# Linear stage of a two-layer conditioned transformer: biases carried by one channel of the norm's output, and another order of stages

## What is computed

```python
# layer 0: adaptive norm, attention with 16 heads of 16 channels, feed-forward 256 -> 1024 -> 256
x = x + attention(_ln(x) * (scale1 + 1) + shift1) * gamma1
x = x + fc2(gelu(fc1(_ln(x) * (scale2 + 1) + shift2))) * gamma2
# layer 1: linear attention
xn = layer_norm(x, norm_g, norm_b)
q = (xn @ Wq + bq); k = (xn @ Wk + bk); v = (xn @ Wv + bv)     # 16 heads of 16 channels
q = softmax(q, over the channels of a head); k = softmax(k, over the tokens)
y = q @ (k.T @ v)                                              # per sequence and head
h = layer_norm(y, sn_g, sn_b) * (1 + scale) + shift
return x + cond * (silu(h) @ out_W + out_b)
```

## Time and profile before

| | us |
|---|---|
| median of three runs | 1304.96 |
| the profiled execution | 1303.32 |
| its span, first to last instruction | 1301.6 |
| TensorE busy (matmuls) | 1165.3 (90%) |
| VectorE busy | 989.4 (76%) |
| ScalarE busy | 802.9 (62%) |
| GpSimd busy | 845.0 (65%) |
| mean granted TensorE clock | 0.971 of full |

### The profile page before, as it was taken

How to read it: one execution, slowest core, us unless ns; L and a number is a source line. 1 busy time by engine, 2 the same in 40 slices (tenths; PEclk the granted TensorE clock), 3 DMA queues, 4 the chain that set the end, 5 groups by cost and what they waited for, 6 DMA issues and landing times. The chain is left out here.

```text
span 1301.6 us, 37761 instructions
## 1 busy us (share of the span) xinstructions
PE 1165.3 (90%) x12137; PEld 838.6 (64%) x12290; DVE 989.4 (76%) x2338; ACT 802.9 (62%) x2144; POOL 845.0 (65%) x1018
## 2 busy tenths in 40 slices
PE   4687999999999964999999999986999999999996
PEld 3466777777777753566666666663666666666663
DVE  6787999999999836656555556435899999999984
ACT  2676778778877741635454544523676776776764
POOL 4567777777777744546666667542476676676667
PEclk8899999999999986999999999997999999999999
DMA  8542222222222221110101010100011111111112
GB/s 277 143 129 49 56 60 59 59 61 56 58 58 61 62 51 53 26 24 17 33 16 32 16 32 17 33 17 1 17 39 38 40 52 37 40 52 39 44 50 74
DMA packets 138368, 67.73 MB, mean 52 GB/s; under 512 B 76352, under 2 KB 137024, under 8 KB 138304
## 3 DMA queue, kind: packets, MB, share of 16 engines
q1 hardware_dynamic: 109904, 40.92, 12.4%
q10 hardware_dynamic: 28400, 25.99, 6.9%
HBM read 41.18 MB, written 8.65 MB: 38 GB/s over the span
## 5 line engine op out<-in xcount | busy, mean ns | idle before, releaser
L1124 PE MATMUL f_ps_y<-w_fc,f_h_split 128*128 128x256 bf16 x1536 | 172.7, 273 | 2.3 <-DVE f_branch L1243 2.3
L1151 PE MATMUL f_ps_h<-f_x_split,w_fc 128*128 128x512 bf16 x737 | 166.5, 383 | 4.5 <-DVE f_biases L1277 1.4
L1124 PEld LDWEIGHTS f_ps_y<-w_fc,f_h_split 128*128 128x128 bf16 x1536 | 150.2, 98 | 23.6 <-issue 3.0
L657 POOL TENSOR_TENSOR e_split<-e_full,e_split 128x1024 bf16<-128x1024 f32 x64 | 136.6, 2134 | 40.0 <-ACT e_full L730 40.0
L1251 DVE TENSOR_TENSOR f_h_split<-f_h,f_h_split 128x512 bf16<-128x512 f32 x64 | 64.2, 1006 | 104.3 <-ACT f_h L1110 104.3
L1151 PEld LDWEIGHTS f_ps_h<-f_x_split,w_fc 128*128 128x128 bf16 x768 | 75.5, 99 | 89.1 <-issue 3.4
L1109 ACT ACTIVATE f_h_split<-f_ps_h,columns 128x512 bf16<-128x512 f32 x128 | 89.2, 697 | 66.5 <-POOL f_h_split L1066 36.4
L790 PE MATMUL ps_s<-qk_t,k_pairs 128*128 128x64 bf16 x3072 | 102.1, 194 | 29.0 <-DMA k_pairs<-qk_t 25.8
L790 PEld LDWEIGHTS ps_s<-qk_t,k_pairs 128*128 128x128 bf16 x3072 | 97.3, 99 | 37.2 <-issue 19.8
L1066 POOL TENSOR_TENSOR f_h_split<-f_h,f_h_split 128x512 bf16<-128x512 f32 x64 | 79.8, 1257 | 36.7 <-ACT f_h L1110 36.7
L1455 POOL TENSOR_TENSOR l_rstd<-l_mean_var,eps_norm 128x2 f32<-128x2 f32 (+1 forms) x73 | 14.3, 196 | 136.9 <-DVE l_mean_var L1648 107.0
(11 more groups left out here) (187 smaller groups left out, 3233.2 us busy)
## 6 DMA issues: line engine op xcount, KB each, us to landing
v_pairs<-v_split SPq DMA_DIRECT2D x128, 66.0 KB, 2.1
k_pairs<-qk_t SPq DMA_DIRECT2D x256, 32.0 KB, 2.2
gain<-gammas SPq DMA_DIRECT2D x64, 128.0 KB, 3.0
f_gain<-gammas ACTq DMA_DIRECT2D x32, 256.0 KB, 4.3
l_gate<-in_cond ACTq DMA_DIRECT2D x128, 64.0 KB, 2.5
out<-x_all ACTq DMA_DIRECT2D x16, 512.0 KB, 3.0
x_all<-in_x SPq DMA_DIRECT2D x13, 512.0 KB, 5.4
fc_full<-in_L_cond_fc_w SPq DMA_DIRECT2D x2, 1024.0 KB, 7.5
```

Of the source, the lines that this page charges most:

```text
L657: pool.tensor_tensor(flat(e_split[a][:, LO]), flat(e_full[:]), flat(e_split[a][:, HI]), ALU.subtract).then_inc(e_lo_made, 1)
L1124: last = pe.matmul(ps_y[:, i], h_split[a][:, hs, f, i * P:(i + 1) * P], m.w_fc2[:, ws, f], start=(f == 0 and k == 0), stop=(f == F_CHUNKS ...
L1151: last = pe.matmul(ps_h[f % 4][:], m.w_fc1[:, ws, c, f * P:(f + 1) * P], x2_split[a][:, xs, c], start=(k == 0 and c == 0), stop=(k == 2 an ...
```

## The change

The first channel of x_hat is no longer written by the norm but held at one: two memsets ahead of the linear stage set it in both buffers, and hat writes channels 1 to 255, with both sides cut into rectangles (5x51 and 3x85). Since x_hat adds up to zero, channel 0 is minus the sum of the others; so the first weight row, times its gain, is subtracted from all the others, and its own place in the weights is taken by the bias. The three bias matmuls per tile and bias_rows' last three parts go. The high and low halves carry the bias like any weight row.

For that, feed_forward_pass loads the first rows of the three matrices to all partitions (three more DMAs, and one for the first gain), VectorE scales them and folds them into the weights, gain included, in float32 (four scalar_tensor_tensor of L1267's kind), and puts the biases into row 0; ScalarE's high half is one copy of 1536 columns, VectorE's low half one subtraction.

In linear_pass the four lists of stages have another order. TensorE's turn_x comes behind qkv and q_kv; VectorE's x3_low behind v_low, and k_low and mask at the end; ScalarE's modulate near the front and k_high, q_copy behind the exponentials; GpSimd's silus ahead of the deviations. The lags stay. Two waits are new: qkv for q_lower of the tile ahead, and v_low for v_high; hat waits for the memsets once.

The diff, cut to its core (the parameter and semaphore declarations are left out, and the waits for the loads, which count ten instead of six):

```diff
--- before.py
+++ after.py
@@ -150,9 +150,8 @@
         self.ones = sb("ones", [P, P], BF16)
-        self.bias_rows = sb("bias_rows", [P, 5 * C], BF16)
-        self.rows_proj, self.rows_out3, self.rows_qv3, self.rows_k3 = (
-            self.bias_rows[:, a * C:b * C] for a, b in ((0, 1), (1, 2), (2, 4), (4, 5)))
+        self.bias_rows = sb("bias_rows", [P, 2 * C], BF16)
+        self.rows_proj, self.rows_out3 = (self.bias_rows[:, a * C:(a + 1) * C] for a in range(2))
 
...
@@ -959,7 +959,8 @@
         biases3 = sb("biases3", [P, 3 * C], F32, 1)[0]
-        biases3_high, biases3_mid = m.w_qkv[:, HI, 0, :], m.w_qkv[:, HI, 1, :]
+        first_rows = sb("first_rows", [P, 3 * C], F32, 1)[0]
+        first_gain = sb("first_gain", [P, 1], F32, 1)[0]
         b_norm3_wide = m.fc_full[:, 6 * C:6 * C + NC_ * P].rearrange("p (c n) -> p c n", c=NC_)
...
@@ -1024,6 +1028,10 @@
                 sp.dma_start(biases3[:, k * C:(k + 1) * C], source[None, :].to_broadcast([P, C])).then_inc(qvk3_here, 16)
+            for k, source in enumerate((wq, wv, wk)):
+                sp.dma_start(first_rows[:, k * C:(k + 1) * C], source[0:1, :].to_broadcast([P, C])).then_inc(qvk3_here, 16)
+            sp.dma_start(first_gain[:], columns[0:1, m.g_norm3_first:m.g_norm3_first + 1].to_broadcast([P, 1]),
+                         allow_slow_non_contiguous=True).then_inc(qvk3_here, 16)
             sp.wait_ge(m.linear_here, 16)
...
@@ -1082,13 +1090,9 @@
                 if isinstance(t.n, int) and t.n == 2:
-                    act.wait_ge(qvk3_here, 16 * 6)
-                    act.wait_ge(norm3_widened, 2)
-                    for c in range(NC_):
-                        act.activation(m.w_qvk3[:, HI, c, 0:2 * C], qvk3_full[:, c, 0:2 * C], ACT.Identity,
-                                       scale=m.g_norm3[:, c:c + 1]).then_inc(qvk3_hi_made, 1)
-                        act.activation(m.w_qvk3[:, HI, c, 2 * C:3 * C], qvk3_full[:, c, 2 * C:3 * C], ACT.Identity,
-                                       scale=minus_g_norm3[:, c:c + 1]).then_inc(qvk3_hi_made, 1)
+                    act.wait_ge(qvk3_folded, 2 * NC_)
+                    act.wait_ge(biases3_placed, 1)
+                    act.activation(m.w_qvk3[:, HI], qvk3_full, ACT.Copy).then_inc(qvk3_hi_made, 1)
 
...
@@ -1261,16 +1265,13 @@
                 if isinstance(t.n, int) and t.n == 2:
-                    dve.wait_ge(qvk3_hi_made, 2 * NC_)
-                    for c in range(NC_):
-                        for cols, g in ((slice(0, 2 * C), m.g_norm3), (slice(2 * C, 3 * C), minus_g_norm3)):
-                            dve.scalar_tensor_tensor(m.w_qvk3[:, LO, c, cols], qvk3_full[:, c, cols], g[:, c:c + 1],
-                                                     m.w_qvk3[:, HI, c, cols], ALU.mult, ALU.subtract)
+                    dve.wait_ge(qvk3_hi_made, 1)
+                    dve.tensor_tensor(m.w_qvk3[:, LO], qvk3_full, m.w_qvk3[:, HI], ALU.subtract)
 
             def carry_biases3(t):
 
                 if isinstance(t.n, int) and t.n == 2:
-                    dve.wait_ge(qvk3_here, 16 * 6)
+                    dve.wait_ge(qvk3_here, 16 * 10)
                     dve.wait_ge(norm3_carried, 1)
...
@@ -1278,17 +1279,18 @@
                     dve.tensor_scalar(biases3[:, 2 * C:], biases3[:, 2 * C:], -1.0, None, ALU.mult
-                                      ).then_inc(biases3_split, 1)
-                    dve.wait_ge(biases3_split, 1)
-                    dve.tensor_copy(biases3_high, biases3[:]).then_inc(biases3_split, 1)
-                    dve.wait_ge(biases3_split, 2)
-                    dve.tensor_copy(m.bias_rows[0:1, 2 * C:], biases3_high[0:1])
-                    dve.tensor_tensor(biases3[:], biases3[:], biases3_high, ALU.subtract).then_inc(biases3_split, 1)
-                    dve.wait_ge(biases3_split, 3)
-                    dve.tensor_copy(biases3_mid, biases3[:]).then_inc(biases3_split, 1)
-                    dve.wait_ge(biases3_split, 4)
-                    dve.tensor_copy(m.bias_rows[32:33, 2 * C:], biases3_mid[32:33])
-                    dve.tensor_tensor(m.bias_rows[64:65, 2 * C:], biases3[64:65], biases3_mid[64:65], ALU.subtract)
+                                      ).then_inc(biases3_turned, 1)
+                    for cols, sign in ((slice(0, 2 * C), -1.0), (slice(2 * C, 3 * C), 1.0)):
+                        dve.tensor_scalar(first_rows[:, cols], first_rows[:, cols], first_gain[:], sign, ALU.mult, ALU.mult
+                                          ).then_inc(first_rows_scaled, 1)
+                    dve.wait_ge(first_rows_scaled, 2)
+                    for c in range(NC_):
+                        for cols, g in ((slice(0, 2 * C), m.g_norm3), (slice(2 * C, 3 * C), minus_g_norm3)):
+                            dve.scalar_tensor_tensor(qvk3_full[:, c, cols], qvk3_full[:, c, cols], g[:, c:c + 1],
+                                                     first_rows[:, cols], ALU.mult, ALU.add).then_inc(qvk3_folded, 1)
+                    dve.wait_ge(biases3_turned, 1)
+                    dve.wait_ge(qvk3_folded, 2 * NC_)
+                    dve.tensor_copy(qvk3_full[0:1, 0, :], biases3[0:1]).then_inc(biases3_placed, 1)
 
...
@@ -1458,8 +1461,8 @@
 
-            pipeline(pool, [(5, softmax), (-1, inverse_deviations), (Y_LAG, last_inverse_deviations),
-                            (10, silus), (12, add)])
+            pipeline(pool, [(5, softmax), (10, silus), (8, last_inverse_deviations), (-1, inverse_deviations),
+                            (12, add)])
 
...
@@ -1530,9 +1533,8 @@
 
-            pipeline(act, [(1, x3_high), (3, v_high), (9, load_gate), (5, k_high), (5, q_copy),
-                           (3, k_exponentials), (9, modulate), (3, q_exponentials), (13, store),
-                           (9, tanhs)])
+            pipeline(act, [(3, v_high), (9, load_gate), (9, modulate), (1, x3_high), (3, k_exponentials),
+                           (3, q_exponentials), (5, k_high), (5, q_copy), (9, tanhs), (13, store)])
 
...
@@ -1598,20 +1600,19 @@
                 reuse(pe, v_lo_made, t, 1)
-                pe.matmul(ps_qv[:], m.ones[:], m.rows_qv3, start=True, stop=False)
+                reuse(pe, q_lowered, t, 1)
                 for i, (xs, ws) in enumerate(SPLITS):
                     for c in range(NC_):
                         last = pe.matmul(ps_qv[:], x3_split[a][:, xs, c], m.w_qvk3[:, ws, c, 0:2 * C],
-                                         start=False, stop=(i == 2 and c == NC_ - 1))
+                                         start=(i == 0 and c == 0), stop=(i == 2 and c == NC_ - 1))
                 last.then_inc(qv_done, 1)
                 reuse(pe, k_exp_made, t, 1, NK)
                 for to in range(NC_):
                     cols = slice(2 * C + to * P, 2 * C + (to + 1) * P)
-                    pe.matmul(ps_k[:, to], m.rows_k3[:, to * P:(to + 1) * P], m.ones[:], start=True, stop=False)
                     for i, (ws, xs) in enumerate(SPLITS):
                         for c in range(NC_):
                             last = pe.matmul(ps_k[:, to], m.w_qvk3[:, ws, c, cols], x3_split[a][:, xs, c],
-                                             start=False, stop=(i == 2 and c == NC_ - 1))
+                                             start=(i == 0 and c == 0), stop=(i == 2 and c == NC_ - 1))
                 last.then_inc(k_done, 1)
...
@@ -1622,8 +1623,8 @@
 
-            pipeline(pe, [(6, k_v_first), (5, turn_kq), (0, turn_x), (6, k_v_second), (11, project), (2, qkv), (7, q_kv),
-                          (Y_LAG, turn_y)])
+            pipeline(pe, [(5, turn_kq), (6, k_v_first), (11, project), (6, k_v_second), (2, qkv), (7, q_kv),
+                          (0, turn_x), (8, turn_y)])
 
...
@@ -1701,6 +1702,7 @@
             def v_low(t):
+                dve.wait_ge(v_hi_made, t.n + 1)
                 reuse(dve, kv_done, t, 4)
...
@@ -1727,8 +1729,11 @@
                 reuse(dve, x_turned, t, 2)
-                dve.tensor_scalar(x_hat[a][:, None, :], t.rows(m.x_all), mean_var[a][:, 0, 0:1], rstd[a][:, 0:1],
-                                  ALU.subtract, ALU.mult).then_inc(x_hat_made, 1)
+                if isinstance(t.n, int) and t.n == 0:
+                    dve.wait_ge(ones_set, 2)
+                dve.tensor_scalar(x_hat[a][:, 1:].rearrange("p (r e) -> p r e", e=51),
+                                  t.rows(m.x_all)[:, 0, 1:].rearrange("p (r e) -> p r e", e=85),
+                                  mean_var[a][:, 0, 0:1], rstd[a][:, 0:1], ALU.subtract, ALU.mult).then_inc(x_hat_made, 1)
 
...
@@ -1736,10 +1741,11 @@
 
-            pipeline(dve, [(-2, statistics), (1, x3_low), (3, k_maxima), (Y_LAG, y_statistics), (3, q_maxima),
-                           (-1, aggregate), (3, q_lower), (3, v_low), (Y_LAG, y_aggregate),
-                           (6, mask), (5, k_low), (-1, hat), (4, total), (Y_LAG, y_hats),
-                           (11, residual)])
+            for a in range(2):
```

(4 more changed lines are left out.)

13 lines of the change are left out of this document (9 added, 4 removed).

## The result

The changed kernel takes **1265.73 us** (median of 4 runs, 1262.96 to 1267.87) against 1305.61 us before, measured beside it: a ratio of 0.9695 with a 95% interval of 0.9671 to 0.972. The forecast was 1275.6 us in a range of 1268 to 1287. The profiled execution took 1262.96 us (span 1261.2), the fastest of the four, as that of before was.

A forecast was written before the change was run, and what follows sets the result against it. TensorE was taken to bound the 54 full steps at 6.05 us each. Gains of 19.4 + 9 + 0.9 = 29.3 us gave 1274.0, on the median's footing 1275.6 us, in a range of 1268 to 1287.

The forecast's parts named there:

- Part 3: New order of stages in the 54 full steps: costs nothing, covered by one us of slack on VectorE.
- part 6: The last 36 us: GpSimd's changed order swaps one wait for another, 0 us, bounds -3 and +3.
- part 2: VectorE's norm write (hat): the cut shape avoids waiting for GpSimd, 0.46 us start to start; earns nothing itself, lets bias-matmul savings be collected.
- part 4: New order in the linear stage's first 11 steps, start included: 9 us gained, bounds 3 and 12.
- Part 1: Three bias matmuls fewer per tile on TensorE: 0.34 us a tile, full step 6.05 to 5.69 us, 19.4 us in all.
- hat 0.4 to 0.55 us: Sign of being right in the profile after: VectorE's norm write takes this long beside GpSimd; near 0.8 would be wrong.
- rival (d): Gate loads' issue on ScalarE, ahead of modulate, delays the k matmuls of every step: slower than before, 1308 us; chance 0.02.
- Part 5: Folding in the feed-forward stage: f_branch starts 1.1 us earlier, shortening a TensorE wait; 0.9 us gained, bounds 0 and 1.2.
- (a): VectorE becomes the bound, since the new hat still waits for GpSimd: full steps gain only 8 to 12 us, 1284; chance 0.16.
- (b): The first steps gain only 3 us, held by the exponentials, k_high, k_low and mask: 1282 us; chance 0.09.
- (c): Both (a) and (b) together, VectorE as bound and first steps gaining little: 1290 us; chance 0.04.

The follow-up runs named there:

- experiment 2: The kernel before with the four new lists of stages and the two waits they need, bias matmuls kept: 1284.06 us, ratio 0.9855.
- experiment 1: The changed kernel with the four lists of stages of before, so the folding without the new order: 1294.08 us, ratio 0.9946.
- experiments 6 to 10: The changed kernel with one engine's old list put back (VectorE 1460.9 us, TensorE 1383.86, ScalarE 1280.5, GpSimd 1274.82), or only TensorE's turn_x moved behind turn_kq (1437.64).

## Why the prediction was wrong, by its own steps

**The step that failed: the order of stages was put at nothing outside the first steps.** Part 3 has it that "the order costs nothing in the full steps", part 6 that it swaps one wait for another at the end. The order alone (experiment 2) brings 0.082 us in each full step, 4.4 us in all, of which the prediction had 1.1, and 3.4 us in the last stage (E 36.8 to 33.4), of which it had nothing. Beside it part 2 has a wrong mechanism, and part 4 a right one with too small a size.

**Part 1 held, in the new order.** 0.34 us a tile from start-to-start distances; 0.323 measured (0.210 + 0.113), 17.4 us over 54 steps. In the old order the same matmuls brought 0.123.

**Part 2: wrong mechanism, and a wrong place in the argument.** The cut changes nothing, since the instruction that reached the chip has one run of 255 on either side; in the old order it takes 0.70 us, as in experiment 1. In the new order hat takes 0.40 in the full steps with or without the cut (experiment 2). The prediction treated the length of hat as what lets part 1 be collected. It is the order that does: fold alone 0.123 a step, with the order 0.323. That GpSimd's instruction lengthens hat was read rightly in the earlier trace rows; that the new shape would take hat out of it was wrong. The sign of being right, "hat 0.4 to 0.55 us", came true in the full steps all the same, by the place of hat in the list: that was luck. In the first steps, where hat still meets GpSimd's instructions, it takes 0.69 to 0.82.

**Part 3: "the order costs nothing in the full steps" had no gain side.** I bounded the full steps by what the bias matmuls could bring (0.39 a step) and priced the order as a risk only. It brings 0.082 us a step: 0.05 by the transposes and the projection's neighbour, 0.03 by the wait ahead of q_kv, of which I had let 0.02 go. What was to be seen in before is that a transpose group took 0.37 or 0.32 us next to k_v; that it takes less next to another transpose, only the new order could show. The placement of the stages itself held: the two added waits cost nothing that a full step shows, the gate loads' issue on ScalarE (rival (d)) nothing either. But I called its cover one us of slack; experiments 6 to 10 show that this holds for the four lists together only. One stage in its old place costs 2.9 us a step.

**Part 4: 9 forecast, 11.6 measured, inside its bounds (3 to 12).** Of the 2.6 us, 1.1 is what I took off the 10.1 that my steps added up to. The start gave 2.2 (2.3 forecast). Of the nine steps, forecast as 5.4, 5.3, 4.6, 4.0, 4.1, 4.4, 5.0, 5.2 and 5.4, the trace has 5.28, 4.36, 3.55, 3.74, 4.25, 4.62, 5.52, 5.52 and 5.63, missing records counted: the last five, placed by VectorE's list, come out 0.1 to 0.5 longer, and the first four 2.4 us shorter together. For the first two I had kept the lower clock. Windows of both traces, cut where the granted clock changes, before first:

```profile
880.90:891.10 10.20, 6.04 (x26) 3.29 (x27) 3.77 (x12) 0.77 (x2) 2.23 (x6) 0.50 0.00 0
891.10:894.60 3.50, 1.38 (x8) 0.71 (x8) 2.64 (x8) 3.37 (x12) 0.74 (x2) 0.99 0.01 2
894.60:898.00 3.40, 2.83 (x18) 1.74 (x16) 0.13 (x2) 0.65 (x3) 0.00 (x0) 0.50 0.02 5
```

```profile
885.50:892.00 6.50, 4.04 (x30) 2.19 (x31) 4.73 (x15) 5.29 (x23) 2.11 (x6) 1.00 0.00 0
```

In both kernels the clock goes from 1.2 to 2.4 GHz 4.2 us behind the first recorded q-and-v matmul (886.85 to 891.1, and 881.28 to 885.5). But before, it fell back from 894.6 to 898.0 us, after 3.5 us in which TensorE was busy for 1.4; in after, TensorE was busy for 4.0 of the next 6.5 us, and the higher level stayed. It stayed in the order-alone kernel too. So the shorter waits kept the level, and of the nine steps only the first ran mostly at the lower one. The second took 4.36 us where I had 5.3 at the lower clock; how much of this 0.9 is the clock, I didn't separate. The third and fourth, which I had placed at the full clock, are 1.0 and 0.3 shorter, by their waits. I had priced the steps' waits and their clock apart. The 6.8 us from which I started runs from the first matmul behind the bias's to the next tile's bias matmul; start to start it is 7.2.

**Part 5: 0.9 forecast, 1.2 measured, at the upper bound.** The single copy and the single pass of after:

```profile
579.96 1.52 ACT L1095 ACTIVATE w_qvk<-fc_full 128x1536 bf16<-128x1536 f32 x1
581.50 1.76 DVE L1269 TENSOR_TENSOR w_qvk<-fc_full,w_qvk 128x1536 bf16<-128x1536 f32 x1 [1.84 <-ACT w_qvk L1095]
...
584.94 5.29 PE L1128 MATMUL f_ps_y<-w_fc,f_h_split 128*128 128x256 bf16 x47
```

are as long as forecast (1.48 and 1.7), and TensorE's wait of 0.89 us is gone: this start of fc2 lies 28.43 us behind the bias sum's in before and 27.38 in after, which is 1.05 of the 1.2 us. The same 1.2 us is in the folding-alone kernel (319.86 from bias sum to turn_x) and not in the order-alone one (321.07).

**Part 6: 0 forecast, 3.6 measured, outside its bound of 3.** I called the last stage "one wait for another". GpSimd's waits for y_aggregate with silus at hand are in the trace of before; one of them, and the second and last of those that are left in after, from GpSimd's timelines:

```profile
1282.73 0.19 POOL L1455 TENSOR_TENSOR l_rstd<-l_mean_var,eps_norm 128x1 f32<-128x1 f32 x1 [1.15 <-DVE l_mean_var L1648]
```

```profile
1243.94 0.19 POOL L1458 TENSOR_TENSOR l_rstd<-l_mean_var,eps_norm 128x1 f32<-128x1 f32 x1 [0.30 <-DVE l_mean_var L1649]
```

Behind the last q-and-v start such waits add up to 3.8 us in before (1.65, 0.67, 1.15 and 0.36) and to 1.4 in after (1.09 and 0.30). In the new list the silus run in that time. With GpSimd's old list alone 2.0 of the 3.6 us are lost again; its two waits for y_aggregate are then 1.14 and 1.11 us, 0.9 more together than in after, so that the waits tell less than half of it. With ScalarE's old list alone E is 33.5 and with TensorE's 34.1, so 0.5 and 1.1 us go with these two. The folding has no part in it but for the bias matmuls: the order alone has 3.4 of 3.8 us, missing records counted.

**What is left: 2.1 us ahead of the bias sum, where nothing of the change works.** Its second VectorE instruction, in before and in after:

```profile
559.68 0.41 DVE L1277 TENSOR_TENSOR f_biases<-f_ps_h,f_biases 128x256 f32<-128x256 f32 x1
```

```profile
557.56 0.41 DVE L1278 TENSOR_TENSOR f_biases<-f_ps_h,f_biases 128x256 f32<-128x256 f32 x1
```

In the other kernels it starts at 557.98 to 560.88 with the old setup and 556.74 to 561.37 with the new one: with both setups it varies by more than 2.1 us, so I don't count it as a gain. Without it the stages sum to 38.3 us, and 1305.0 - 38.3 = 1266.7 against the median of 1265.7.

Of the terms alone, then: full steps +2.5 us, first steps and start +2.6, last stage +3.6, feed-forward +0.3, together 9.0 of the 9.9 us. No single one is large, and any of the three larger ones at its forecast would have left the time inside the range. The lower edge of 1268 already had every gain at its bound (21 + 12 + 1.2 + 3 = 37.2 us); the full steps (21.9) and the last stage (3.6 to 3.8) went past theirs, the first steps came close to theirs, and all lie on one side because each of my zeros and roundings was made against the change.

Two slips in my range and base weigh little: its upper end, 1287, leaves out the last stage's bound of -3 (1289 with it), and the nine steps of before are 51.40 us long by the rows, not 51.2.

**The rivals.** (a) is real, but it is the folding without the new order (1294 us); in the change itself TensorE has no regular wait for y_hats. (b), (c) and (d) didn't occur.

## What to carry to other kernels

A matmul taken off a full TensorE was worth its start-to-start distance here only with the engine 0.3 us behind relieved at the same time. The relief came from an order of stages, and the two together brought 10.8 us more in the full steps than each on its own would sum to (54 x (0.323 - 0.123)). Price an order from both sides: the neighbours of short groups on TensorE, and every idle time in front of an instruction whose successors are ready. Ask of each term that is taken into a matmul whether it reaches the result at all; the key's bias didn't. And the lists of the four engines are one design: put back one at a time, each costs 9 to 195 us. What one new list alone does among three old ones was not run.
